# Router logits taken from the raw sums, with each expert's router weights centred on the chip

## The reference

```python
xn = _layernorm(x, axis=-1)
x = x + gnn(xn, src, dst, ...) + mix(xn[None], ...)[0]
x = x + ffn(_layernorm(x, axis=-1)[None], router_w, w1, b1, w2, b2)[0]

def _layernorm(x, axis=-1, eps=1e-05):
    m = jnp.mean(x, axis=axis, keepdims=True)
    v = jnp.var(x, axis=axis, keepdims=True)
    return (x - m) / jnp.sqrt(v + eps)

def _moe(tokens, router_w, w1, b1, w2, b2):
    logits = tokens @ router_w.T                    # 8 experts
    probs = softmax(logits)
    rw, re = top_k(probs, 2)
    rw = rw / rw.sum(-1)                            # weights of the two
    out = tokens
    for e in range(8):
        y = gelu(tokens @ w1[e] + b1[e]) @ w2[e] + b2[e]
        out = out + combine[:, e:e + 1] * y
    return out
```

## Time and profile before

| What | us |
|---|---|
| median of 3 runs | 480.64 |
| range of the runs | 477.76 to 482.14 |
| the profiled execution, its own time | 476.46 |
| its span, first to last instruction | 474.7 |
| PE busy | 432.2 (91%) |
| DVE busy | 317.6 (67%) |
| ACT busy | 281.7 (59%) |
| POOL busy | 180.6 (38%) |
| mean granted TensorE clock | 0.97 of full speed |

### The profile page before, as it was taken

The page is one execution under the profiler, slowest core; times in us unless marked ns, Lnnn a source line. Parts: engine busy times, 40 slices in busy tenths (PEclk is TensorE's granted clock), DMA queues, the critical chain, the costliest instruction groups (busy, mean ns, idle before and its releaser), DMA issues.

```text
span 474.7 us, 10025 instructions
## 1 busy us (share of the span) xinstructions
PE 432.2 (91%) x3259; PEld 320.2 (67%) x3259; DVE 317.6 (67%) x900; ACT 281.7 (59%) x625; POOL 180.6 (38%) x235
## 2 busy tenths in 40 slices
PE   1899999989999999999998999965799999999993
PEld 0786787766566666555555565642699999899982
DVE  3687869867776777777751688875266666666661
ACT  1756555656777777677772587830676776444441
POOL 5056695564111111111110014685144544445443
PEclk9999999999999999999999988965999999999998
DMA  8836012946778979888776001232366565566750
GB/s 215 182 120 195 25 27 73 287 90 124 127 148 148 162 174 184 184 146 143 125 135 125 1 6 49 73 86 70 92 186 198 184 195 163 146 179 175 188 157 16
DMA packets 113379, 62.91 MB, mean 133 GB/s; under 512 B 89675, under 2 KB 103942, under 8 KB 113328
## 3 DMA queue, kind: packets, MB, share of 16 engines
q1 hardware_dynamic: 104144, 47.04, 45.5%
q0 software_dynamic: 8368, 14.38, 9.6%
q10 hardware_dynamic: 816, 0.85, 0.7%
HBM read 22.96 MB, written 21.36 MB: 93 GB/s over the span
## 4 chain that ended last, share of the span: by engine, by line
PE 77%; DMA 6%; ACT 5%; DVE 4%; issue 3%; POOL 3%; SPq 1%; POOLq 0%; ACTq 0%; DVEq 0%
PE bank L1294 12%; PE bank L1503 11%; PE bank L1514 11%; PE bank L1245 9%; PE bank L1325 4%; PE bank L1212 4%; PE bank L1221 4%; PE bank L1188 4%; PE bank L1492 3%; DMA region_a<-region_a 3%; PE bank L1228 2%; DMA rows<-in_x 2%; PE bank L1440 2%; PE bank L1305 2%; PE bank L1512 1%
## 5 line engine op out<-in xcount | busy, mean ns | idle before, releaser
L629 ACT CAST region_a<-bank 128x500 bf16<-128x500 f32 (+1 forms) x175 | 112.2, 668 | 46.1 <-PE bank L1245 41.9
L1294 PE MATMUL bank<-region_a,region_z 125*64 125x500 bf16 (+1 forms) x525 | 69.8, 361 | 2.4 <-DMA region_a<-region_a 2.4
L1245 PEld LDWEIGHTS bank<-region_a 128*128 128x128 bf16 x625 | 41.2, 101 | 42.6 <-issue 31.0
L1245 PE MATMUL bank<-region_a 128*128 128x125 bf16 x625 | 64.8, 220 | 1.7 <-ACT region_a L629 1.4
L1503 PE MATMUL bank<-region_a,region_c 128*128 128x128 f32 x496 | 65.8, 275 | 0.0
L1514 PE MATMUL bank<-region_c,region_a 128*128 128x256 f32 x248 | 63.7, 379 | 0.0
L1503 PEld LDWEIGHTS bank<-region_a,region_c 128*128 128x128 f32 x496 | 60.2, 191 | 0.4
L715 ACT ACTIVATE region_a<-bank,region_c 128x128 f32<-128x128 f32 x124 | 39.0, 367 | 32.9 <-PE bank L1503 29.9
L525 POOL COPY wide<-den 125x256 f32<-125x256 f32 x25 | 12.9, 516 | 119.4 <-DVE den L937 119.4
L1157 DVE COPY region_c<-region_w 128x1026 f32 x62 | 43.2, 697 | 16.8 <-issue 16.7
L565 POOL DMA_INDIRECT xs_next<-region_a x31 | 31.1, 1003 | 45.1 <-DVE region_a L1168 37.4
(11 more groups left out here) (226 smaller groups left out, 771.8 us busy)
## 6 DMA issues: line engine op xcount, KB each, us to landing
region_a<-xs_next SPq DMA_DIRECT2D x31, 259.0 KB
region_w<-in_w SPq DMA_DIRECT2D x4, 1024.0 KB, 9.4
region_a<-xs SPq DMA_DIRECT2D x31, 131.0 KB
rows<-in_x SPq DMA_DIRECT2D x5, 560.0 KB
xs_next<-null SPq DMA_DIRECT2D x8, 259.0 KB, 2.7
xs_next<-null SPq DMA_DIRECT2D x1, 1554.0 KB, 9.6
xs<-null SPq DMA_DIRECT2D x8, 131.0 KB, 2.3
xs<-null SPq DMA_DIRECT2D x1, 786.0 KB, 6.5
```

Of the source, the lines that this page charges most:

```text
L629: nc.scalar.copy(to, count_bank(n)[:, 0:w * TP].rearrange("p (c t u) -> p c t u", c=w, t=NT)).then_inc(adj_done, 1)
L1245: last = nc.tensor.matmul(count_bank(n)[:, (c - lo) * TP:(c - lo + 1) * TP], loh[:, t % 2, c, :], koh[:, t % 2, c, 0:TP], start=True, stop ...
L1294: last = nc.tensor.matmul(block_out(b), zparts[:, t, part, :], adjT[0:TP, t % 2, lo:hi, 0:TP], start=False, stop=False, skip_group_check=True)
```

## The change

The logits of normalised tokens are (x2 - mean) / deviation times the router weights. The changed kernel first subtracts from each expert's router weights their mean over the 256 features, so that the token's mean drops out of the product. Then it takes the logits from the raw sums `x2`. The division by the deviation is positive and the same for all experts of a token, so it does not alter which are the largest; it is applied only to the difference of the two largest, before the exponential. The centring is two products with a tile of ones on PE (`ones_f`, filled by POOL) and two instructions of DVE. The transposes wait for `x2_done` and not for `tk_done`. With that the orders of ACT and DVE and the numbers of zero products ahead of the loop are altered:

```diff
+        ones_f = r.take(P, P)
...
             nc.gpsimd.memset(adj[:, 1, :, TP:P], 0.0).then_inc(pad_zeroed, 1)
+            pool.wait_ge(keys_done, 2)
+            nc.gpsimd.memset(ones_f, 1.0).then_inc(ones_set, 1)
             split_z(G - 1)
             set_tables()
...
+            copy_tokens(0)
             token_scale(0)
             normalize_tokens(0)
-            copy_tokens(0)
+            copy_tokens(1)
             token_scale(1)
             for g in range(NR):
                 n = ROUT[g][1] - ROUT[g][0]
-                if g + 1 < NR:
-                    normalize_tokens(g + 1)
                 act.wait_ge(diff_done, g + 1)
                 nc.scalar.activation(ex[:, 0:n], ex[:, 0:n], ACT.Exp).then_inc(ex_done, 1)
                 if g + 1 < NR:
-                    copy_tokens(g + 1)
+                    normalize_tokens(g + 1)
                 if g + 2 < NR:
+                    copy_tokens(g + 2)
                     token_scale(g + 2)
...
+            def centre_router():
+                dve.wait_ge(rw_summed, 1)
+                for k in range(2):
+                    last = nc.vector.scalar_tensor_tensor(rw[:, k, :], h0[:, 0:NX], -1.0 / D, rw[:, k, :], ALU.mult, ALU.add)
+                last.then_inc(rw_centred, 1)
...
+            centre_router()
             dve.wait_ge(g2_ready, 2)
...
                 if g >= 3:
                     dve.wait_ge(tk_done, ROUT[g - 3][1])
+                    dve.wait_ge(t3_ready, g - 2)
                 dve.wait_ge(g3_ready, hi)
...
-                nc.vector.tensor_tensor(ex[:, 0:n], top[:, 0:n, 1], top[:, 0:n, 0], ALU.subtract).then_inc(diff_done, 1)
-                dve.wait_ge(diff_done, g + 1)
+                chain(nc.vector.tensor_tensor(ex[:, 0:n], top[:, 0:n, 1], top[:, 0:n, 0], ALU.subtract))
+                nc.vector.tensor_tensor(ex[:, 0:n], ex[:, 0:n], rstd2[:, g % 2, 0:n], ALU.mult).then_inc(diff_done, 1)
...
             for g in range(NR):
+                choose(g)
                 if g + 1 < NR:
                     scale(g + 1)
-                choose(g)
                 if g + 2 < NR:
                     add_graph(g + 2)
                 weigh(g)
...
+            pe.wait_ge(qn_done, NT)
+            pe.wait_ge(ffn_in, 16)
+            pe.wait_ge(ones_set, 1)
+            for k in range(2):
+                last = nc.tensor.matmul(h0[:, 0:NX], ones_f, rw[:, k, :], start=(k == 0), stop=(k == 1))
+            last.then_inc(rw_summed, 1)
...
             graph2(m1, (7, 8, 9, 10, 11, 24), 3)
+            pe.wait_ge(rw_centred, 1)
             graph2(h0, range(12, 22), 5)
...
-                pe.wait_ge(tk_done, hi)
+                pe.wait_ge(x2_done, hi)
...
-                        last = nc.tensor.transpose(ps, xb[:, lo + j, k * P:(k + 1) * P], ident[0:TP, 0:TP])
+                        last = nc.tensor.transpose(ps, x2[:, g % 3, j, k * P:(k + 1) * P], ident[0:TP, 0:TP])
...
-                if g == 0:
-                    pe.wait_ge(ffn_in, 16)
-                else:
+                if g >= 1:
                     pe.wait_ge(lg_read, g)
...
             graph3(0)
-            keep_clock(lg_ps, 7)
+            keep_clock(lg_ps, 3)
             graph3(1)
-            keep_clock(lg_ps, 14)
             transpose_tokens(0)
-            keep_clock(lg_ps, 4)
+            keep_clock(lg_ps, 3)
             logits(0)
```

More of the change, by code:

```diff
@@ L310, in build @@
             "xt_ready", "xT_done", "w_copied", "hid_ready", "gelu_done", "y_ready", "ys_done"))
+        ones_set, rw_summed, rw_centred = sem("ones_set"), sem("rw_summed"), sem("rw_centred")
         passed, restored, below_done = sem("passed"), sem("restored"), sem("below_done")
```

## The result

The changed kernel takes 491.8 us in the median (490.45 to 494.82, four runs) against 480.09 for the kernel before (477.76 to 482.14, four runs). The ratio is 1.0254, interval 1.0197 to 1.0311: slower by 11.7 us. The forecast was 489.1 us with a range of 482 to 494, and slower. The ratios leave out executions in which the chip ran in a slower state, such as one of 707.4 us at a granted clock of 0.56 in the first series of the kernel with the root first.

What follows compares the result with a forecast made beforehand. The prediction took DVE's delivery of group 3's slots to POOL as the bound; a late scale(0) and rounds of about 10.44 us through three engines moved the 25th send by 8.5 us, giving 489.1 us, range 482 to 494.

Steps and rivals of the forecast that it cites:

- Where the bound sits: POOL's thirteen gapless sends: the end is DVE's delivery of group 3's slots plus a constant; first send 308.66 before, 317.2 forecast.
- The late first scale: DVE's scale(0) waits for ACT's root, now behind copy and table load: 271.8 where it ran at 268.65.
- The round: From scale(g) to scale(g+1) through DVE, PE and ACT: 2.31 + G + 4.24 = 10.44 us with G = 3.89.
- the walk: Start times followed group by group: scale(1) 280.9, scale(4) 311.8, slots of group 3 at 316.3, POOL's send at 317.2.
- G: PE's graph3 and eight zero products in each round: 3.89 us, mean of three passes, with 2.80 and 4.44 as ends.
- low clock throughout: Rival on PE's clock: G = 4.44 in all rounds, 10.99 a round, +10.7, 491.3 us; chance 0.08.
- The multiply by the deviation: One more small DVE instruction per group: 0.08 us, at most 0.2, times four groups.
- The centring: PE's two fp32 products, four records: 0.47 us on the path, bounds 0 and 1.0; DVE's two instructions cost nothing.
- POOL's fill: POOL's fill of 128x128, 0.21 us, covered by POOL's 0.88 idle time ahead of the attention part's first spread.
- No slower, because DVE hides the loop: Rival at DVE's wait at L1040: scale never late, 8.90 a round, 478.4 to 482.1 us; chance 0.11.
- ceiling: Most the change can win if all DVE's stalls go: -2.98 + 0.47 + 4 x 0.08 = -2.2 us.
- The dearer table switch: Rival on ACT: table load first lets the copy run out, up to 1.3 a round, +5, 494 us; chance 0.02.

Runs made afterwards that it cites:

- the kernel with the root first: Changed kernel with ACT's token_scale(g) put back ahead of copy_tokens(g), all else as changed: 476.67 us, in a second series 478.53 us.
- the first attempt to improve on it: The kernel with the root first, with weigh(g) moved ahead of add_graph(g+2) on DVE: 490.63 us, ratio to before 1.0241.
- the best version: The kernel with the root first, plus weigh(g) ahead of add_graph(g+2) and ACT's exponential of g ahead of copy_tokens(g+1), eight zero products kept: 475.26 us.

## Why the prediction was right

The mechanism was the one forecast. Its size was not: the change cost 11.7 us where 8.5 were forecast, and the state of the clock that came true was not the one on which the forecast stood. The steps can be set side by side. Positions are less the 2.0 us by which the changed kernel's profile was late already ahead of the routing.

| Step | forecast | measured |
|---|---|---|
| `scale(0)` | 271.8 | 272.0 |
| round into `scale(1)` | 9.1 | 9.60 |
| rounds into `scale(2)` and `(3)` | 10.4 each | 11.11 each |
| round into `scale(4)` | 10.0 | 10.62 |
| `scale(4)` to the last slot of group 3 | 4.46 | 4.69 |
| thirteen sends | 17.98 | 18.43 |
| 25th send, later by | 8.5 | 11.8 |

*Where the bound sits* held: the end follows the first send of group 3, from which POOL sends without a gap. POOL's last sends took somewhat longer (up to 1.87 us from one to the next), 0.45 in all. What I had not seen is that DVE's pace before was not its own alone: the chain that ended last before goes round through PE and ACT, from one `logits` (279.80) over `graph3`, zero products, transposes and copy to the next (289.49) and the one after (298.91), 9.69 and 9.42 us, and ACT's root of the next group stood behind each of these copies already. Three of the four stalls of `scale` before follow such a root.

*The late first scale* held to 0.2 us, and the run with the root first takes it back (270.90, of which 1.8 were there ahead of the routing; the centring explains the 0.5 that is left over 268.65).

*The round* held in each part but one. From `scale` to `graph3` 2.31 to 2.38 (2.31 forecast), from the copy to the next `scale` 2.97 (2.97), into `scale(1)` 1.55 (1.67). One wording was off: the adds behind `scale(g)` free the banks for `graph3(g+2)`, not for `graph3(g+1)`; the walk had it right. The mis-sized term is G, PE's `graph3` and eight zero products, with the transposes behind it: I took 3.89, the mean of three passes, of which one was at full clock. Measured from the start of `graph3` to ACT's copy: 5.74, 5.80 and 5.76 where I had 3.89 + 1.27 = 5.16, and 5.28 for three tiles in place of 4.74. That is 0.6 us in each of four rounds, 2.4 of the 3.3 missing. G itself was 4.45, 3.88 and 4.44; in the round of 3.88 the transposes took the low clock instead (1.83 in place of 1.23). In size it is the case "low clock throughout" (4.44 + 1.27 = 5.71, +10.7 in all), to which I had given 0.08. That 489.1 still came within 2.7 us of the result owes something to luck: the four passes before were two at full clock and two at the low one (I left out the fourth, of three tiles, 2.66 us from 301.19), and the changed kernel had none at full clock. I had named why the clock would be lower (PE idles longer than before) and yet let the old passes set the mean. In the run with the root first, where PE waits less, three of the four such passes are at full clock; that fits this reason, but no run tests it alone.

*The multiply by the deviation* held: from the subtraction to the cast behind it DVE takes 0.27 (302.32 to 302.59) where it took 0.19 (302.70 to 302.89 before), the 0.08 of the forecast. In the changed kernel this stands ahead of the wait for `scale`, where it costs nothing.

*The centring* held: 0.51 us on PE, nothing that the runs can tell. *POOL's fill* was taken as covered; in the changed kernel POOL is again idle, 0.89 us, ahead of the step behind it, as in the earlier trace rows.

*No slower, because DVE hides the loop*, was rightly the rival of the other side: the root-first kernel comes near its ceiling of -2.2 (-2.0). In part that is luck. The ceiling counted the stall of 0.28 at 308.96, which lies behind the slots of group 3, so it should have been -1.9; DVE's rounds came out at 8.4 to 8.7 where I had 8.90; and in the end POOL's own queue took over, from group 2 on. I had put the point from which the rival decides at G under 2.35 or a root not held back by the copy. The second half of that is what the run shows. The first half did not hold: removing the zero products brought G to about 2.0, and yet DVE was late in each round, because ten transposes then took 2.18 to 2.35 us at the low clock (I had counted 1.27 up to the copy) and because I had left out the chain over two rounds.

*The dearer table switch*: the load starts 0.01 us behind the copy ahead of it (303.80 + 0.39 = 304.19) and the root right at the end of its load (304.20 + 1.28 = 305.48, root at 305.50), so the rule of the Trainium skill, "ScalarE: Activation LUTs", section "What ACT_TABLE_LOAD costs", that a switch costs about twice the load, again does not show in the trace.

## What to carry to other kernels

Where engines run written orders and wait on one another, draw the loop that an instruction closes when it is moved, not only what it gains: here moving an eviction ahead of a root made three engines wait in turn, in each round DVE 1.8 to 3.6 us for ACT and ACT 3.7 to 6.4 for PE, and a second such loop appeared in the first attempt to improve on it. Put what another engine waits for ahead of what waits for another engine. And two reorderings must be judged together: DVE's new order is worth 3 to 5 us with one order of ACT and 30 us with the other.

## What the runs showed of the hardware that I had not expected

Products that exist only to hold the clock give back most of what they cost, even on the path. Without them the granted clock stayed at 1.2 GHz through much of the routing, and twenty records of 8 columns took up to 4.21 us in place of 2.35, ten transposes 2.35 in place of 1.23. Over the same stretch, without them and with them (columns as in the earlier trace rows):

```profile
276.00:320.00 44.00, 37.10 (x195) 29.81 (x195) 33.32 (x219) 27.25 (x50) 14.35 (x12) 0.58 0.14 37
```

```profile
276.00:320.00 44.00, 37.32 (x234) 24.64 (x235) 32.03 (x209) 25.64 (x47) 14.34 (x12) 0.84 0.13 34
```

The granted clock is 0.58 in place of 0.84, and PE is busy as long with 39 records fewer. So the removal of products that took 12.6 us in the chain (3.51, 2.95, 3.25 and 2.89 in the four rounds) made the routing only 2.1 us shorter, where I had expected 7 to 10. With four in place of eight, in the best version, the routing was 2.7 us longer in the profile, at a granted clock of 0.70 in place of 0.90 from 276 to 310; the times of the runs don't tell these two apart.
